# One order for TensorE's steps rewritten, and its side products issued as four column tiles

## The reference

```python
def ffn(x):                       # weights rounded to -1, 0, 1
    h = relu(x @ quantize(W1).T + b1)          # 128 -> 512
    return h @ quantize(W2).T + b2             # 512 -> 128
def attn(x):                      # 16 heads of 8 channels
    q, k, v = rope(x @ Wq.T + bq), rope(x @ Wk.T + bk), x @ Wv.T + bv
    return softmax(q @ k.T / sqrt(8)) @ v  # per head, then @ Wo.T + bo
x = x + 0.5 * ffn(layernorm(x))
x = x + attn(layernorm(x))
x = x + 0.5 * ffn(layernorm(x))
```

## Time and profile before

| what | value |
|---|---|
| time, median of 3 runs | 584.28 us (583.87 to 587.52) |
| profiled execution | 578.99 us |
| its span | 577.2 us |
| PE busy | 518.6 us, 90% |
| DVE busy | 396.2 us, 69% |
| ACT busy | 369.8 us, 64% |
| POOL busy | 220.6 us, 38% |
| granted TensorE clock | 0.994 of full speed over the span |

### The profile page before, as it was taken

The page is one execution under the profiler, slowest core; times in us unless marked ns, Lnnn a source line. Parts: engine busy times, 40 slices in busy tenths (PEclk is TensorE's granted clock), DMA queues, the critical chain, the costliest instruction groups (busy, mean ns, idle before and its releaser), DMA issues.

```text
span 577.2 us, 8687 instructions
## 1 busy us (share of the span) xinstructions
PE 518.6 (90%) x3230; PEld 237.4 (41%) x3230; DVE 396.2 (69%) x579; ACT 369.8 (64%) x432; POOL 220.6 (38%) x291
## 2 busy tenths in 40 slices
PE   6659999889999999999999888989899989898986
PEld 4446635233535344343535233423334333432346
DVE  4874976767786687657776687668856776678314
ACT  4669675677475765767475666576566657576751
POOL 1554372527342546427340545153613531103202
PEclk9998999999999999999999999999999999999999
DMA  7056038012800344012800362034502360000000
GB/s 226 30 182 147 1 112 219 2 29 100 204 1 20 111 132 92 2 46 101 203 1 21 111 162 60 2 112 131 110 1 57 148 147 2 21 1 3 2 18 19
DMA packets 19177, 44.60 MB, mean 77 GB/s; under 512 B 2624, under 2 KB 5440, under 8 KB 18112
## 3 DMA queue, kind: packets, MB, share of 16 engines
q1 hardware_dynamic: 18464, 43.53, 27.4%
q10 hardware_dynamic: 672, 0.52, 0.3%
HBM read 20.45 MB, written 18.87 MB: 68 GB/s over the span
## 4 chain that ended last, share of the span: by engine, by line
PE 71%; DVE 16%; ACT 4%; DMA 4%; issue 4%; POOL 1%; SPq 1%; POOLq 0%; DVEq 0%; ACTq 0%
PE heads_acc L556 20%; PE unit L541 13%; PE unit L526 12%; DVE maxima L837 10%; PE side L611 9%; PE side L605 5%; PE side L594 3%; DMA q_stack<-max_T 3%; ACT hidden L737 2%; PE heads_acc L619 2%; PE unit L611 1%; PE side L590 1%; PE side L599 1%; PE side L575 1%; DVE attn_out L850 1%
## 5 line engine op out<-in xcount | busy, mean ns | idle before, releaser
L837 DVE TENSOR_REDUCE maxima<-unit 128x2 f32<-128x1024 f32 x256 | 307.1, 1221 | 129.9 <-PE unit L526 129.7
L747 ACT ACTIVATE probs<-unit 128x1024 f32<-128x1024 f32 x256 | 261.5, 1025 | 128.1 <-PE unit L541 126.8
L541 PE MATMUL unit<-q_stack,k_stack 64*128 64x512 f32 x512 | 125.6, 488 | 25.1 <-DVE maxima L837 18.8
L556 PE MATMUL heads_acc<-probs,v_heads 128*32 128x512 f32 x1024 | 136.4, 605 | 1.0 <-ACT probs L747 1.0
L526 PE MATMUL unit<-k_stack,q_stack 62*128 62x512 f32 x512 | 115.9, 448 | 0.0
L526 PEld LDWEIGHTS unit<-k_stack,q_stack 62*128 62x128 f32 x512 | 48.2, 184 | 104.8 <-issue 87.6
L541 PEld LDWEIGHTS unit<-q_stack,k_stack 64*128 64x128 f32 x512 | 47.7, 183 | 91.2 <-DVE maxima L837 43.1
L1001 POOL TENSOR_SCALAR max_parts<-maxima 128x16 fp32r<-128x16 f32 x32 | 6.6, 205 | 192.7 <-DVE maxima L837 192.7
L611 PE MATMUL side<-w_q,hidden 128*128 128x128 f32 x416 | 59.3, 287 | 0.0
L611 PEld LDWEIGHTS side<-w_q,hidden 128*128 128x128 f32 x416 | 50.1, 191 | 15.5 <-issue 14.6
L737 ACT ACTIVATE hidden<-side,b_col 128x512 f32<-128x512 f32 x49 | 33.8, 690 | 18.1 <-PE side L605 18.1
(11 more groups left out here) (142 smaller groups left out, 472.4 us busy)
## 6 DMA issues: line engine op xcount, KB each, us to landing
k_scratch<-k_parts SPq DMA_DIRECT2D x16, 512.0 KB, 2.9
q_scratch<-q_parts SPq DMA_DIRECT2D x16, 512.0 KB, 2.9
k_stack<-k_scratch SPq DMA_DIRECT2D x14, 512.0 KB, 7.1
q_stack<-q_scratch SPq DMA_DIRECT2D x14, 512.0 KB, 9.0
resid<-in_x SPq DMA_DIRECT2D x8, 256.0 KB, 6.9
k_swap<-k SPq DMA_DIRECT2D x16, 128.0 KB, 2.3
q_swap<-q SPq DMA_DIRECT2D x16, 128.0 KB, 2.3
out_y<-resid SPq DMA_DIRECT2D x7, 256.0 KB, 2.0
```

Of the source, the lines that this page charges most:

```text
L541: mm = pe.matmul(to[:, e, :], k_stack[part, quad // NQ % 2, pair, kt * P:(kt + 1) * P], q_stack[part, quad // NQ % 2, pair, :], start=True ...
L556: mm = pe.matmul(heads_acc[32 * j:32 * j + 32, :], v_heads[:, b % 2, at, ODD * odd:ODD * odd + 32], probs[:, burst % RING, j, :], start=(k ...
L747: act.activation(probs[:, burst % RING, 2 * pp:2 * pp + 2, :], unit_of(USE_OF["exp", n]), ACT.Exp, scale=SCALE).then_inc(s_exp, 1)
L837: dve.tensor_reduce(maxima[:, quad % 2, :, r], unit_of(USE_OF["max", k]), AX_X, ALU.max).then_inc(s_max, 1)
```

## The change

Two things are changed. The two strings that set the order are written anew, with the same words in other places: `e` and `m` stand in groups of one to six, other words in groups between them. And every side product but the transposes is issued as four matmuls of 32 output columns, one for each quarter of the array's columns, in place of one of 128 columns: `COLUMNS` is the list of the four quarters. The tail's products (L669 on) stay as they are, and so do POOL's and SP's orders.

```diff
+COLUMNS = [slice(32 * c, 32 * c + 32) for c in range(4)]
 PE_STEADY = """
-e m ffn1_T
-e pv m ffn1_up0
-heads_copy1@-1 e m ffn1_up1
-e pv m heads_T1@-1
-e m ffn1_up2 ffn1_stats@5
...
+ffn1_T m e
+heads_copy1@-1 m pv ffn1_up0 e m ffn1_up1
+e m
+e ffn1_stats@5 heads_T1@-1
...
+e pv m m ffn1_down0 ffn1_down1 ffn1_down2 m
+e m ffn1_down3 pv
+e max_T2
...
                 elif name in ("q", "k"):
                     pe.wait_ge(s_xT, index + 1)
-                    pe.matmul(to, w_proj[:, "qk".index(name), :], x_T[:], start=True, stop=True).then_inc(s_qk_psum[name], 1)
+                    for cols in COLUMNS:
+                        mm = pe.matmul(to[cols, :], w_proj[:, "qk".index(name), cols], x_T[:], start=True, stop=True)
+                    mm.then_inc(s_qk_psum[name], 1)
...
                     for n, part in enumerate((x_hi, x_lo)):
-                        mm = pe.matmul(to, w1_q[:, arg * P:(arg + 1) * P], part[:], start=(n == 0), stop=(n == 1))
+                        for cols in COLUMNS:
+                            mm = pe.matmul(to[cols, :], w1_q[:, arg * P + cols.start:arg * P + cols.stop], part[:],
+                                           start=(n == 0), stop=(n == 1))
...
                     for n in range(FT):
-                        mm = pe.matmul(to[:, arg * P:(arg + 1) * P], hidden[:, n, arg * P:(arg + 1) * P],
-                                       w2_q[:, n, :], start=(n == 0), stop=(n == FT - 1))
+                        for cols in COLUMNS:
+                            mm = pe.matmul(to[cols, arg * P:(arg + 1) * P],
+                                           hidden[:, n, arg * P + cols.start:arg * P + cols.stop],
+                                           w2_q[:, n, :], start=(n == 0), stop=(n == FT - 1))
```

More of the change, by code:

```diff
@@ L55 @@
 PE_FIRST = """
[L56 to L71, removed]
-e m
-e pv m
-heads_copy0 e m
-e pv m heads_T0
-e m
[L77 to L87, removed]
+attn_T@1 k@1 e m m q@1
+e
+e
+e m m ffn1_T m pv
+e
+e ffn1_up0 ffn1_stats@5 pv m m pv max_T1 m ffn1_up1 m
+e ffn1_up2
+e
+e m m ffn1_up3
+e
+e attn_stats
+e m pv ffn1_down0 ffn1_down1 pv m m
+e ffn1_down2
+e ffn1_down3
+e max_T2 m
+e pv m m pv
+heads_copy0 pv m v m e
+e m
+e
+e pv
+e m pv max_T3 m
+e attn_T
+e
+e pv heads_T0
+e m
+e
+e m m k pv m
+e m pv
+e m m
+e pv max_T4 m
+e q m pv m
+e
 """
 PE_STEADY = """
-e m ffn1_T
-e pv m ffn1_up0
-heads_copy1@-1 e m ffn1_up1
-e pv m heads_T1@-1
-e m ffn1_up2 ffn1_stats@5
[L95 to L104, removed]
-e pv m
[L106 to L119, removed]
+ffn1_T m e
+heads_copy1@-1 m pv ffn1_up0 e m ffn1_up1
+e m
+e ffn1_stats@5 heads_T1@-1
+e pv m
+e m max_T1 pv ffn1_up2 m
+e m out_T pv ffn1_up3 m
+e
+e out
+e ffn2_stats
+e pv m m ffn1_down0 ffn1_down1 ffn1_down2 m
+e m ffn1_down3 pv
+e max_T2
+e m pv m
+e attn_stats
+e v
+heads_copy0 pv m m pv ffn2_T e m ffn2_up0
+e
+e m ffn2_up1
+e pv heads_T0
+e m m ffn2_up2
+e pv max_T3
+e m m ffn2_up3 pv
+e m ffn2_down0
+e m m ffn2_down1 ffn2_down2 ffn2_down3
+e m
+e pv attn_T
+e m
+e k pv
+e m m pv max_T4
 e m q
-e pv m
+e m pv
 """
@@ L598, in side_work @@
                     for t in range(T):
-                        mm = pe.matmul(to[:, t * P:(t + 1) * P], lhs[:, t * P:(t + 1) * P], w_proj[:, w, :],
-                                       start=True, stop=True)
+                        for cols in COLUMNS:
+                            mm = pe.matmul(to[cols, t * P:(t + 1) * P], lhs[:, t * P + cols.start:t * P + cols.stop],
+                                           w_proj[:, w, :], start=True, stop=True)
                     mm.then_inc(s_v_psum if name == "v" else s_out_psum, 1)
```

## The result

The changed kernel takes 546.17 us (median of 4 runs, 544.88 to 546.74) where the kernel before, beside it on the same chip, took 584.08 (578.63 to 587.52): a ratio of 0.9377 with a 95% interval of 0.931 to 0.9444. It is faster, by more than the forecast of 561 us, and lies where the rival "all of it arrives" (549 or 543) put it.

The account below looks back on a forecast made before the run. PE was taken as the bound (busy 90% of the span), DVE second. Savings of 11.4 us in batches 1 to 3 and 10.9 in the others gave 584.3 - 22.3, rounded to 561 us; range 541 to 587.

Parts of the forecast that it names:

- all of it arrives: Whole kernel: idle time stays as it is, all 35.4 us saved become time, 549 us or 543; chance 0.20.
- The entry price: On PE: each run costs a fixed entry and exit, 0.19 us for `e` and `m`, 0.12 for 32-column tiles.
- PE work saved: Eight batches: fewer runs save PE 35.4 us, 6.2 in each of batches 1 to 3.
- What waits: Batches: idle time grows from 2.6 to about 5 us in 1 to 3; elsewhere 0.65 of 16.7 us saved arrives.
- The reading of the ring at one place: Behind the second `up`: a unit is free 1.8 us after its step began, so PE waits at least 0.35.
- The ratios 0.53 and 0.62: Fall in batch time per fall in PE busy time: 3.88 of 7.25 us (batch 1 to 4), 1.63 of 2.64 (4 to 6).
- Nothing else on the path: Prologue and other engines: some ten more entries cost 0 to 1.5 us, taken as 0.
- The rival of issue: Runs of `down`, `v`, `out`: instruction issue limits tiles, a `down` costs 1.98 us not 0.90; 597 to 610 us; chance 0.09.
- The ring takes it all back: Batches 1 to 3: PE waits for DVE's maxima, they end at 64 us instead of 61, total 582; chance 0.14.

Follow-up runs that it names:

- no_joins: Changed kernel, tiles kept, words moved in the steady string so that no two products of 32 columns are neighbours: 590.67 us, ratio 1.0102 to the kernel before.
- order_only: Changed kernel with the new strings but every side product whole instead of in four tiles: 545.65 us, ratio 0.9383 to the kernel before.
- tiles_only: Kernel before, old order kept, side products as four tiles of 32 columns: 593.38 us, ratio 1.0168; run once more for its profile, 592.52 us.
- whole_prologue: Changed kernel with whole products in the prologue and beside the first maxima, tiles kept in the batches: 541.19 us, ratio 0.9285 to the kernel before.
- 2 x 2 table: Medians with the new order: batches whole, 545.65 us (prologue whole) and 551.71 (prologue tiled); batches tiled, 541.19 and 546.17.

## Why the prediction was right, and where it was off

**The entry price, right.** 0.19 us for a run of `e` and `m` and 0.12 for one of 32-column products, both worked out from the earlier trace rows, give what `no_joins` added (4.34 for 4.45), what `order_only` lacks (1.3 for 1.51 in batch 1, 58.27 against 56.76) and what `tiles_only` saved (0.7 for 0.70). That joined products pay no entry, which no row of before showed, stands in the `v` and `pv` rows: 0.20 us less than whole products, 0.14 less than tiles of another width.

**PE work saved, right in its kind, 7.1 us too large.** 35.4 were forecast for the eight batches, 28.3 came: 5.54 and 6.23 for the 6.2 of batches 1 and 3, but 2.19 for 3.9 in batch 4 and 0.61 for 1.7 in batch 7, both with a clock of 0.97 for which I had no term. Some of the rest are short waits between the steps of a group, counted as busy: the third step behind the second `up`, for which I had worked out a wait of at least 0.35, starts 0.61 after the `m` before it, not 0.34:

```profile
137.19 0.51 PE L527 MATMUL unit<-k_stack,q_stack 62*128 62x512 f32 x2
137.80 0.50 PE L542 MATMUL unit<-q_stack,k_stack 64*128 64x512 f32 x2
```

**What waits: the step that failed.** I let the idle time of batches 1 to 3 grow from 2.6 to 5 us and took 0.65 of the saving elsewhere, so 13.1 of 35.4 were to go to the ring. Instead all idle time fell, by 12.2: this term was 25.3 us off, and with the 7.1 above it makes up the 18.2 between 22.3 forecast and 40.5 measured for the batches. The reading of the ring at one place was near (0.27 where at least 0.35 was worked out). What I did not do was to look at what the waits of before were for. 18.8 us of them were for maxima, 8.2 for `attn_out`, 5.9 for a transfer; in the new order they come to 9.3, 0.2 and 1.3, and `order_only` shows that it is the order that does it. I had even written that the long groups give DVE time to read, and gave it no number. The ratios 0.53 and 0.62, from which I took 0.65, came from batches with fewer products but the same old order, and so said nothing of a new one. `no_joins` shows that it could have gone as I feared, and worse: there the idle time of a full batch is 5.6.

**Nothing else on the path: wrong, by 5 us before the first `m`.** I costed the prologue at 0 to 1.5, looking only at PE's entries. Of the 5.0 us before the first `m`, 1.6 are a wait for `resid` that ends later (in `whole_prologue` it ends 1.2 later too, so the tiles alone are not to blame) and 3.3 the last long `down`: 2.46 of them the stop, the rest a clock that stays low for longer (0.52 from 48 to 51 us, where it was 1.00 before). The 2 x 2 table has 5.0 to 6.1 on the medians. The 1.1 of the tail are not shown to be the change's. So the forecast was off by terms that partly cancelled: the waits 25 us too dear, the busy time 7 and the stretches around the batches 8 too cheap, 10 in sum. The prediction's own sum is 562, not the 561 it was rounded to; of the 15.8 us from there to 546.2 the other 5.7 lie between profiles and medians and stay open. That the time fell inside 541 to 587 is owed to the width of that range and to this cancelling as much as to the price of the entries.

**The rival of issue, refuted where it stood.** A `down` in a run costs 0.90 (153.61 to 154.51), and 128 matmuls in the prologue 3.70 (from 18.32 us on); 1.98 was the price of the rival. The Trainium skill's 62 ns for a matmul decoded by the sequencer ("TensorE: Matmul & The Clock Gate", section "Wait — 56ns, not 53.3ns?") would have made it so; here 32 matmuls in 0.90 us are 28 ns each. The 25 ns that it gives otherwise come, as an estimate, to 0.80 for a `down` and not to the 0.90 of the prediction, so these rows do not test them. Yet the sign of that worry was right in another shape: more instructions do cost time here, not at each one, but, as far as the rows can tell, in stops, the four longest of them behind one long dense stretch.

**The ring takes it all back: not seen.** DVE's share rose from 69% to 72%, and PE waits for its maxima half as long as before.

## What to carry to other kernels

Count how often an engine changes between kinds of work and what one change costs, but treat the order that saves changes as a new order: list what the old one waits for, by releaser, and ask of each wait what stands ahead of it now. Split instructions only where the split buys something (here, next to a product of the same width): a split elsewhere cost no PE time in the batches here, but it lengthens the program, and in the dense prologue the split products went with stops of the engine. Test the two halves of a change apart before keeping both; here one half alone gives the same time with 4,512 fewer instructions.

## What the runs showed of the hardware

- Products of 32 and of 64 columns do not join: `v` and `pv` start 0.14 us further apart than with equal tiles, which pay no entry between them.
- PE can stop for 0.7 to 4.7 us with no semaphore to wait for, between a weight load and its matmul or in the middle of a product. They are seen only in kernels with many tiles of 32 columns; the four longest (2.46 to 4.72) lie behind the long tiled `down` of the prologue, four shorter ones (0.72 to 2.00) in the batches.
- A stop or a long wait is often followed by the lower clock. After the wait of 4.24 us above, in `tiles_only_look`, PE's clock in three windows of 3 us (the figure behind POOL's count):

```profile
111.00:114.00 3.00, 2.55 (x14) 1.03 (x14) 1.23 (x1) 1.66 (x2) 0.00 (x0) 0.50 0.00 0
114.00:117.00 3.00, 2.54 (x14) 0.83 (x6) 1.27 (x2) 1.66 (x3) 0.00 (x0) 0.56 0.00 0
117.00:120.00 3.00, 2.99 (x20) 1.25 (x20) 2.11 (x2) 1.26 (x2) 0.00 (x0) 1.00 0.02 5
```

0.50 is 1.2 GHz, and the first `pv` there takes 1.86 us to the next product where it took 0.99 before. But the 2.46 us stop in the changed kernel was followed by a clock of 1.00, and the 2.00 us in `whole_prologue` by one of 0.50 (218 to 220 us), so the length of a stop alone does not tell which comes.
